# The head of a chunked scan taken pair by pair, with inputs and result laid out in DRAM as their tiles lie in SBUF

## The reference, cut to what matters

```
layer 0: x += gate * (linear recurrence over time of rmsnorm(mod(x)) @ B, @ C, + D)
         x += gate * score * expert[argmax](mod(x))             # 8 experts, 128 -> 256 -> 128
layer 1: q, k = silu(h Wq), silu(h Wk); v = h Wv                # h = mod(x); 16 heads of 64
         lr, wd = rates from sigmoid(h Wlr), sigmoid(h Wbeta), mean over a chunk
         for each of 8 chunks of 64 tokens:                     # carry W_in, W_out: 64 x 64 a head
             p_q, p_k = softmax(W_in q), softmax(W_in k);  o = p_q W_out
             G = gradient through the softmax of k with v and W_out
             W_out = W_out * wd_out + lr_out * p_k^T v;  W_in = W_in * wd_in + lr_in * G^T k
         x += gate * (o Wo)
         x += gate * top-2 of 8 experts (capacity 256, 128 -> 512 -> 128)
```

## Time and profile before

| | us |
|---|---|
| median of 3 runs | 822.17 (820.05 to 823.3) |
| the profiled execution | 820.11 |
| its span | 818.4 |
| TensorE busy | 706.1 (86%) |
| VectorE busy | 639.6 (78%) |
| POOL busy | 571.4 (70%) |
| ACT busy | 477.2 (58%) |

### The profile page before, as it was taken

How to read it: one execution, slowest core, us unless ns; L and a number is a source line. 1 busy time by engine, 2 the same in 40 slices (tenths; PEclk the granted TensorE clock), 3 DMA queues, 4 the chain that set the end, 5 groups by cost and what they waited for, 6 DMA issues and landing times.

```text
span 818.4 us, 34170 instructions
## 1 busy us (share of the span) xinstructions
PE 706.1 (86%) x14849; PEld 648.5 (79%) x14850; DVE 639.6 (78%) x1039; ACT 477.2 (58%) x764; POOL 571.4 (70%) x425
## 2 busy tenths in 40 slices
PE   4668677736989999999999999999999999786997
PEld 3358567736879999899988899889999888675897
DVE  5993754448879999899988999999998998866215
ACT  4745333424846775586767567666757765648510
POOL 4811177173778899889898988878888878732750
PEclk9775689959999999999999999999999999986999
DMA  9741354310060000000000000000000000062128
GB/s 230 199 108 39 78 120 97 74 48 13 24 191 8 10 8 7 7 6 11 7 6 7 20 2 3 11 10 3 4 16 4 4 17 16 4 206 77 51 78 274
DMA packets 60959, 42.89 MB, mean 52 GB/s; under 512 B 21776, under 2 KB 53664, under 8 KB 60816
## 3 DMA queue, kind: packets, MB, share of 16 engines
q1 hardware_dynamic: 57232, 34.00, 15.1%
q0 software_dynamic: 3296, 6.76, 3.7%
q10 hardware_dynamic: 288, 0.01, 0.0%
HBM read 26.65 MB, written 14.09 MB: 50 GB/s over the span
## 4 chain that ended last, share of the span: by engine, by line
PE 70%; issue 11%; DVE 7%; POOL 5%; ACT 4%; DMA 2%; DVEq 0%; POOLq 0%; ACTq 0%; SPq 0%
PE psum L1872 19%; PE psum L1927 8%; PE psum L1972 7%; PE psum L1905 7%; PE psum L1963 4%; PE psum L1920 4%; PE psum L1934 4%; PE psum L1942 3%; ACT arena L1064 2%; PE psum L1913 2%; PE psum L2223 2%; POOL arena L564 1%; PE psum L1810 1%; POOL y_rows L703 1%; PE psum L1736 1%
## 5 line engine op out<-in xcount | busy, mean ns | idle before, releaser
L1872 PE MATMUL psum<-hT,w_qkv 128*128 128x128 f32 x1408 | 173.4, 280 | 2.3 <-DVE arena L1418 1.9
L1872 PEld LDWEIGHTS psum<-hT,w_qkv 128*128 128x128 f32 x1408 | 164.2, 194 | 5.3 <-DVE arena L1418 2.1
L610 POOL TENSOR_TENSOR arena<-arena,small 128x1024 f32<-128x1024 f32 x56 | 106.0, 1914 | 48.9 <-DVE small L1431 48.9
L589 POOL TENSOR_TENSOR arena<-arena 128x1024 f32<-128x1024 f32 x56 | 106.7, 1905 | 13.0 <-ACT arena L947 12.4
L575 POOL TENSOR_TENSOR arena<-arena 128x1024 f32<-128x1024 f32 x56 | 106.5, 1902 | 0.0
L1424 DVE TENSOR_REDUCE small<-arena 128x16 f32<-128x1024 f32 x60 | 73.2, 1219 | 9.1 <-ACT arena L936 6.8
L614 POOL TENSOR_TENSOR arena<-arena 128x1024 f32<-128x1024 f32 x28 | 65.8, 2352 | 17.5 <-DVE arena L1451 17.5
L1412 DVE TENSOR_REDUCE small<-psum 128x16 f32<-128x1024 f32 x60 | 72.8, 1216 | 2.2 <-PE psum L1972 2.2
L916 ACT ACTIVATE arena<-psum 128x1024 f32<-128x1024 f32 x28 | 28.7, 1025 | 72.4 <-PE psum L1872 72.4
L1418 DVE TENSOR_TENSOR arena<-psum,small 128x1024 f32<-128x1024 f32 x60 | 70.5, 1215 | 0.1
L1905 PE MATMUL psum<-arena 64*128 64x64 f32 x1344 | 61.5, 230 | 8.1 <-issue 6.7
(11 more groups left out here) (323 smaller groups left out, 1620.9 us busy)
## 6 DMA issues: line engine op xcount, KB each, us to landing
y_rows<-hT SPq DMA_DIRECT2D x8, 512.0 KB
arena<-y_rows SPq DMA_DIRECT2D x8, 512.0 KB, 7.3
o_rows<-arena SPq DMA_DIRECT2D x9, 256.0 KB
x_sb<-in_L_attn_u SPq DMA_DIRECT2D x8, 256.0 KB, 6.0
arena<-in_W_inT SPq DMA_DIRECT2D x16, 128.0 KB
arena<-in_W_out SPq DMA_DIRECT2D x64, 32.0 KB
h_rows<-arena SPq DMA_DIRECT2D x4, 512.0 KB, 3.5
h_rows<-hT SPq DMA_DIRECT2D x8, 256.0 KB, 2.3
```

The source lines that it names most:

```text
L589: pool.tensor_tensor(x3, x3, lr[:, tile_of(t) * 32 + k * H:tile_of(t) * 32 + k * H + H].unsqueeze(2).to_broadcast([P, H, D]), ALU.mult).th ...
L610: pool.tensor_tensor(z4, z4, r3.unsqueeze(3).to_broadcast([P, 8, 2, CH]), ALU.mult).then_inc(done, 1)
L1872: mm = pe.matmul(ps[bank][:, p * P:(p + 1) * P], w_qkv[:, j * HD + p * P:j * HD + (p + 1) * P], hT[:, at:at + P], start=True, stop=True)
```

## The change

In DRAM, x, the result, both layers' expert weights, w_o and the scan's initial states now lie as their tiles lie in SBUF, so that a row of a partition is one run; the host lays them out and turns the result back. That makes 4 DMAs of the 8 for x, 8 of the 80 for the states, 1 of the 4 for w_o, and 8 of the 16 for the result.

The head of the scan takes pair 0 of group 0 alone as soon as its own gather has landed (`first_back`) and the other three pairs together after it. Norm and modulation of group 0 move from ACT to VectorE. ACT makes two roots (pair 0, pairs 1 to 3), loads the Tanh table, and goes on with tanh; group 1's root comes one turn later with a table load on either side. TensorE runs 12 warm-up products, then interleaves transposes and products. The k product of step 1 goes to another PSUM bank (`k_bank`), so it need not wait for step 0's logits to be read. POOL takes over `group_take` of groups 1 and 2, issues 12 instead of 16 gathers ahead of its loop, and two each in turns -1 to 2 behind the normalisations. Group 1's transposes, hT, tokens and sums come one turn later (`early_of`).

```diff
+        def early_of(i, ahead, n=NC):
+            return 1 if i + ahead == 5 else group_of(i, ahead, 2, n)
+        def rows_in(c):
+            return c // 2 * 64 + (64 if c % 2 else 48)
+        def k_bank(t):
+            return 0 if t == 1 else 3
...
@@ sync
             def load_x(bp):
-                for be in range(2):
-                    sp.dma_start(x_sb[be * CH:(be + 1) * CH, bp * W8:(bp + 1) * W8].rearrange("p (t c) -> p t c", c=C),
-                                 A["L0_attn_u"][2 * bp + be].rearrange("(t p) c -> p t c", p=CH)).then_inc(x_in[bp], 16)
+                sp.dma_start(x_sb[:, bp * W8:(bp + 1) * W8], A["x_rows"][:, bp * W8:(bp + 1) * W8]).then_inc(x_in[bp], 16)
...
+            sp.dma_start(w_o[:, :], A["Wo_rows"]).then_inc(a1_w, 16)
             def load_w_in(bp):
+                sp.dma_start(w_in[bp], A["W_in_rows"]).then_inc(w_set, 16)
             def load_w_out(bp):
+                sp.dma_start(w_out[bp], A["W_out_rows"]).then_inc(w_set, 16)
...
+                half = slice(n * (W8 // 2), (n + 1) * (W8 // 2))
+                sp.dma_start(A["out"][:, half], x_sb[:, half]).then_inc(out_sem, 16)
@@ gpsimd
+            def group_take(c):
+                b3, x3, gates = group_tiles(c)
+                pool.wait_ge(group_taken, c)
+                pool.wait_ge(back_in[c % 2], rows_in(c))
+                chain.link(pool.tensor_tensor(b3, b3, tile_scores(c), ALU.mult))
+                chain.link(pool.tensor_tensor(b3, b3, gates, ALU.mult))
+                pool.tensor_tensor(x3, x3, b3, ALU.add).then_inc(group_taken, 1)
-            for n in range(4 * BP):
+            for n in range(2 * BP):
                 gather_back(n)
+            group_take(1)
+            for n in range(2 * BP, 3 * BP):
+                gather_back(n)
+            group_take(2)
...
             for i in range(-1, TU - 1):
-                if i + 17 < T:
+                if 3 <= i and i + 17 < T:
                     gather_back(i + 17)
...
                 normalise_p(i + 1, 0, pq_norm)
                 normalise_p(i + 1, 1, pk_norm)
+                if i < 3:
+                    gather_back(2 * i + 14)
+                    gather_back(2 * i + 15)
@@ scalar
+            act.activation(junk, ln_eps, ACT.Sqrt)
+            first_root(0, 1, 1)
+            first_root(1, BP, 2)
+            act.activation(junk, ln_eps, ACT.Tanh)
+            q_tanh(0); k_tanh(0); group_tanh_of(0); q_tanh(1); k_tanh(1); exponentials(0, 0)
...
+                if i == 0:
+                    group_root(1)
+                    act.activation(junk, ln_eps, ACT.Tanh)
@@ vector
+            dve.wait_ge(first_back, 16)
+            chain.link(first_take(0, 1))
+            first_measure(0, 1); first_norm(0, 1); first_hT_of(0).then_inc(group_hT, 1)
+            dve.wait_ge(back_in[0], rows_in(0))
+            first_take(1, BP).then_inc(group_taken, 1)
+            first_measure(1, BP); first_norm(1, BP); first_hT_of(1).then_inc(group_hT, 1)
+            q_silu(0); first_hT_of(2); first_hT_of(3).then_inc(group_hT, 1)
+            k_silu(0); q_silu(1); maxima(0, 0); group_rates_out(0); maxima(0, 1)
+            centre(0, 0); centre(0, 1); k_silu(1); group_measure(1)
+            add_up(0, 0); add_up(0, 1); invert(0); group_rate(1)
@@ tensor
+            keep_warm(12, ps[1][:, 0:P])
+            first_turn(0); pe.wait_ge(group_hT, 1); project(0, 0, 1, pe_pq)
+            first_turn(1); project(0, 1, 3, pe_pk); first_turn(2); first_turn(3)
+            pe.wait_ge(group_hT, 2); pe.wait_ge(silu_q, 1); project(1, 0, 1, pe_pq); group_tokens(0)
+            pe.wait_ge(silu_k, 1); logits_of(0, 0); group_sum(0); logits_of(0, 1)
+            pe.wait_ge(group_rates, 1); project(1, 1, k_bank(1), pe_pk)
+            pe.wait_ge(z_centered, 1); pe.wait_ge(silu_q, 2); pe.wait_ge(silu_k, 2); logits_of(1, 0)
+            pe.wait_ge(z_centered, 2); logits_of(1, 1)
+            for i in range(2, TZ):
+                turned, tokens, summed = early_of(i, 2), early_of(i, 1, NC - 1), early_of(i, 0, NC - 1)
```

More of the change, by code:

```diff
@@ L997, in group_score @@
                 last.then_inc(group_scored, 1)
[L999 removed]
+            act.activation(junk, ln_eps, ACT.Sqrt)
+            first_root(0, 1, 1)
+            first_root(1, BP, 2)
+            act.activation(junk, ln_eps, ACT.Tanh)
+            q_tanh(0)
+            k_tanh(0)
+            group_tanh_of(0)
+            q_tanh(1)
+            k_tanh(1)
+            exponentials(0, 0)
+            for i in range(0, TU + 1):
                 if 0 <= i - 1 < TU:
                     k_tok_out(i - 1)
[L1002 to L1004 removed]
+                exponentials(i, 1)
+                if 1 <= i and i + 1 < TZ:
                     k_tanh(i + 1)
[L1006 to L1007 removed]
+                if i == 0:
+                    group_root(1)
+                    act.activation(junk, ln_eps, ACT.Tanh)
                 if 0 <= i - 1 < TU:
@@ L1466, in gate_y @@
                 dve.tensor_tensor(y_gated, y_bank(t), rows1(GA, t % BP), ALU.mult).then_inc(y_scaled, 1)
-            group_take(0)
-            group_measure(0)
-            group_rate(0)
-            group_take(1)
-            group_measure(1)
-            group_take(2)
-            for i in range(-3, TU - 1):
+            dve.wait_ge(first_back, 16)
+            chain.link(first_take(0, 1))
+            first_measure(0, 1)
+            first_norm(0, 1)
+            first_hT_of(0).then_inc(group_hT, 1)
+            dve.wait_ge(back_in[0], rows_in(0))
+            first_take(1, BP).then_inc(group_taken, 1)
+            dve.wait_ge(group_taken, 1)
+            first_measure(1, BP)
+            first_norm(1, BP)
+            first_hT_of(1).then_inc(group_hT, 1)
+            q_silu(0)
+            first_hT_of(2)
+            first_hT_of(3).then_inc(group_hT, 1)
+            k_silu(0)
+            q_silu(1)
+            maxima(0, 0)
+            group_rates_out(0)
+            maxima(0, 1)
+            centre(0, 0)
+            centre(0, 1)
+            k_silu(1)
+            group_measure(1)
+            add_up(0, 0)
+            add_up(0, 1)
+            invert(0)
+            group_rate(1)
+            for i in range(-1, TU - 1):
                 if i >= 0:
@@ L2253, in layouts @@
     a["L1_b1_cols"] = t(np.asarray(inputs["L1_ffn_b1"]).reshape(E, F1 // P, P), 2, 0, 1).reshape(P, -1)
-    a["W_inT"] = t(w_in, 1, 2, 0)
-    a["W_out"] = t(w_out, 1, 0, 2)
+    twice = lambda x: np.ascontiguousarray(np.concatenate([x.reshape(P, -1)] * 2, axis=1))
+    a["W_in_rows"] = twice(w_in.reshape(D, HP, 2, D).transpose(2, 3, 1, 0))
+    pairs = w_out.reshape(D, 2, 2, 2, 2, D).transpose(3, 4, 0, 1, 2, 5)
+    a["W_out_rows"] = twice(np.stack([np.stack([pairs[q ^ r, r] for r in range(2)], axis=3) for q in range(2)]))
+    wo = t(inputs["L1_attn_Wo"], 1, 0).reshape(4, 2, 2, D, C).transpose(1, 2, 3, 0, 4)
+    a["Wo_rows"] = np.ascontiguousarray(np.stack([np.stack([wo[q ^ r, r] for q in range(2)], axis=1) for r in range(2)]).reshape(P, HP * C))
+    for l in range(2):
+        a[f"L{l}_W1_rows"] = t(inputs[f"L{l}_ffn_W1"], 1, 0, 2).reshape(P, -1)
+        w2 = np.asarray(inputs[f"L{l}_ffn_W2"])
+        a[f"L{l}_W2_rows"] = t(w2.reshape(E, -1, P, C), 2, 0, 1, 3).reshape(P, -1)
+    a["x_rows"] = t(np.asarray(inputs["L0_attn_u"]).reshape(BP, 2, NC, CH, C), 1, 3, 0, 2, 4).reshape(P, T * C)
     return a
```

266 lines of the change are left out of this document (114 added, 152 removed).

## The result

The changed kernel takes 814.62 us (four runs, 812.83 to 815.39) where the kernel before takes 821.97 beside it (820.05 to 823.3): ratio 0.9901, 95% interval 0.9873 to 0.9929, faster by 7.35 us. On another chip the same pair gave 0.9879 (0.9846 to 0.9912). The forecast was 817.0 in a range of 810 to 821.5.

The account below looks back on a forecast made before the run. TensorE was taken to bound the scan's steps and latency its start; -1.3 -0.6 -0.7 -2.8 +0.5 +0.6 = -4.3 gave 815.8 or 817.9 by base, and the forecast was set at 817.0, range 810 to 821.5.

Parts of the forecast that it names:

- First loads: Kernel start: one DMA per input pair lets the weights TensorE waits for land sooner, -1.3 us (bounds 0.7 and 2.0).
- Initial states: First layer's gathers: 80 state DMAs become 8, so SP's queue no longer slows a gather, -0.6 us (bounds 0 and 1.2).
- Last store: Kernel end: 16 DMAs become 8, one issue fewer behind the last addition, -0.7 us (bounds 0.3 and 1.2).
- Head, the gain: Scan start: VectorE begins after the first pair's gather; step 0's logits 6.3 us earlier, step 1's 7.4 earlier.
- Given back, first part: VectorE before step 1's maxima: group 1's moments, sums and rate, plus 1.3 us contention, cut the gain to 5.0.
- Given back, second part: Group 3's late gathers hold ACT for 3 us, with hT behind; the gain shrinks from 4.7 to about 1 at k_silu(3).
- Third, the stall: TensorE's 3.70 us stall before the transposes at 233.05 falls partly into an existing wait: -2.8 us (bounds 1 and 5).
- Rival A: Scan head: early start survives, gathers 14 and 15 land before ACT asks and the stall goes; 813 us, chance 0.30.
- Fourth: POOL's first four turns: eight gathers issued where it issued four, +0.5 us (bounds 0 and 2.6).
- tokens: Group 1's tokens and sums move one turn later, into one where TensorE is full, +0.6 us (bounds 0 and 1.6).
- Rival B: Front: big loads back to back fill the DMA engines and instructions come late; slower, 826 us, chance 0.08.
- Rival C: Front's gain is lost in VectorE's chain and the stall keeps its length; -1.7 in all, 820.5 us, chance 0.20.

Follow-up runs that it names:

- the vector first: Changed kernel with group 3's gathers ahead of POOL's taking of group 2 and the conditioning vector first in the inputs' queue: ratio 0.9902 to the kernel before.
- the layouts alone: Kernel before with the new loads and stores and the old head, against the kernel before: ratio 0.9964 on the second chip, 0.9979 on the fourth.
- the gathers ahead: Changed kernel with group 3's gathers issued ahead of POOL's taking of group 2, against the kernel before: 0.9825 (second chip), 0.9846 (fourth, 805.15 us).
- the head alone: Changed kernel with the old loads and stores, against the kernel before: ratio 0.9859 on the second chip, 0.9924 on the third.

## Why the prediction was right, and where its terms were off

**First loads, -1.3.** Too large. The columns moved from 7.90 to 7.32 on the first chip and not at all on the fourth (7.31 and 7.32). In all traces they start at 6.94 to 7.90 with the old loads and at 7.30 to 7.32 with the new, 7.58 with the vector first. At the states' reading no lead beyond the spread between traces is left. The step that failed is the assumption that issues and packets in front of the weights set their landing: the weights now go out at 1.27 instead of 2.28, and on the fourth chip neither the load of the weights into TensorE (7.29 against 7.31) nor the columns started sooner.

**Initial states, -0.6.** The queue's hold of 10.39 is gone, but of the lead of 2.12 at the first expert gather (97.69 to 95.57, fourth chip) 2.27 arrive at the first return gather, so this stage gave 0.15. A gather of 1.46 to 1.48 stands some 8 us behind the first one in every trace from the first, third and fourth chip, with the new loads too (at 103.5 to 105.6): the 1.48 of the earlier trace rows had nothing to do with SP's sixteen issues.

**Last store, -0.7.** 1.0, in each trace with the new layout. I had an issue gone and no change in what one costs; it fell from 0.616 to 0.333 as well. The three terms sum to -2.6, and the layouts alone measured -3.1 and -1.7. The sum fits, but of its terms the traces bear out only this one.

**Head, the gain.** First product 6.6 earlier forecast, 6.55 in the first pair of traces; logits of step 0 6.3 against 6.5; logits of step 1 7.4 against 8.1. These steps hold, and so does the 12.50 to 6.11 and 6.25 of the fourth chip.

**Given back, first part.** Forecast 5.0 at the k product of step 2, found 8.0. The 5.0 itself isn't what the listed terms give: 1.25, 2.4, 0.7 and 1.3 sum to 5.65, which would leave 1.8 of the 7.4, and the prediction shows no working for the difference. Two terms were wrong. VectorE's moments and sums, which I counted as new work in front of the maxima, fell into time in which VectorE had been idle before: 1.12, 0.48 and 1.92 us,

```profile
199.87 1.23 DVE L1412 TENSOR_REDUCE small<-psum 128x16 f32<-128x1024 f32 x1 [1.12 <-PE psum L1972]
201.57 1.23 DVE L1412 TENSOR_REDUCE small<-psum 128x16 f32<-128x1024 f32 x1 [0.48 <-PE psum L1972]
206.98 1.22 DVE L1424 TENSOR_REDUCE small<-arena 128x16 f32<-128x1024 f32 x1 [1.92 <-ACT arena L936]
```

which is the kernel before, waiting twice for TensorE's logits of 2.90 and once for ScalarE. And the 1.3 for contention at the rate's last operation did not come, by 0.01 us of order (0.16 at 189.40). The Trainium skill (GPSIMD Engine Reference, section Specifications) has POOL contend with VectorE instructions of two SBUF inputs. The rows agree where POOL's operation was already running: 0.99 with the gathers ahead, 1.45 in the earlier trace rows. The rule was right and the order in time was not.

**Given back, second part.** The mechanism held, and the size of the hold: ScalarE was held 3.25 (forecast 3), hT followed, and from step 1's normalisation to k_silu(3) the lead fell from 8.1 to 3.0, by 5.1 where I had 3.7. k_silu(3) is 3.0 earlier, I had said 1. The run with the gathers ahead takes 3.0 of the loss away (56.28 against 59.24), which shows the cause.

**Third, the stall.** This is the term that was mis-sized. I had the transposes 2.8 earlier, on the ground that part of TensorE's stall would fall into a wait that is there anyway. They came 6.1 earlier in the first trace (67.78 to 61.65 from the first return gather), since VectorE's lead of 3.0 and the stall's 3.70 added up, less 0.6 that they now start further behind their operand. The upper bound of 5 was too low as well. And nothing was counted for the lower clock behind the stall, 1.2 us up to the logits of step 3. Rival A's reason (TensorE passes before the writes flow) doesn't fit: the writes began at 212.35, 9.7 ahead of the transposes, about as before (10.3). Why TensorE has no such stall with the new head is open: in eight of nine traces with it there is none over 1 us up to step 3's logits, and in the ninth one of 1.88 in a place where the old head had none. In the trace of after a packet of instructions ended at 220.25, 1.8 ahead of the transposes at 222.09, so there it was in time; the one that ended at 225.79 was not, and behind it came the stall of 1.88. TensorE's program is another one with the new head, which no run separates.

**Fourth, +0.5, and tokens +0.6.** No run separates them. POOL is busier by 8 us in the whole span (571.4 to 579.5) and the head alone still nets 6.2.

**The sum.** In two parts the forecast was layouts -2.6 and head -1.7 (-2.8 +0.5 +0.6). Measured: layouts -1.7 and -3.1, head -6.2 on the third chip, whole -7.35 on the first. The result came 2.4 under the forecast because the head kept more than I gave it, near Rival A's 813, though not by A's way: the hold of ScalarE was there. Rival B fell: no product of TensorE waits over 1 us under the name issue in the first 60 us. Its weight loads do, 5.1 where it was 4.7, at a place where the product beside them waits for POOL; it is 5.1 in the second trace of before too. Rival C fell with the head alone.

That 817.0 lies as near as it does is partly luck. The early terms were too large (-1.9 for first loads and states, of which the traces show 0.6 and 0.15 at most), the stall's was too small (-2.8 against 6.1), and in the one pair of traces from the first chip the head's lead of 7.4 at the logits of step 3 is gone by the last projection (548.64 and 548.95), which no term foresaw.

## What to carry to other kernels

A wait that precedes another isn't simply subtracted from it: to size a stall that no operand explains, take it away in the kernel before (here by spreading the writes around it, worth 0.9967 by itself) and only then sum. Look in the list of DMA queues for the packet of instructions ahead of it, and count the lower clock behind it too (here 1.2 us on top of 2.7). When work is moved ahead of a point, look for the idle time that it will fill; 3.5 us of "new" work on VectorE cost nothing here because VectorE had stood still for as long in the same turn. And when gathers are moved out of the way of a head, ask who needs the last of them: keeping group 3's ahead took ScalarE's wait of 3 us away and gave the fastest kernel of this study.

## What the runs showed of the hardware that I had not expected

One chip took 860 us for the kernel that takes 818 to 822 on the three others, and most of the time lies in one stage. With the layouts alone the first return gather was at 187.24 there and at 160.97 on the fourth chip: 26 of the 37 us between these two traces, with 4 more in the turns of the scan and 7 behind them, where the same kind of wait stands again. At 111 to 126 us three engines stood still together, ScalarE and VectorE with their inputs long made, TensorE behind VectorE:

```profile
121.49 1.14 ACT L828 ACTIVATE arena<-psum,route 128x128 f32<-128x128 f32 x4 [10.39 <-remote]
125.51 0.69 DVE L1283 COPY arena<-psum 128x512 f32<-128x512 f32 x1 [19.11 <-remote]
126.26 3.78 PE L1789 MATMUL psum<-arena 128*128 128x128 f32 x16 [13.63 <-DVE arena L1283]
187.24 0.99 POOL L529 DMA_INDIRECT arena<-o_rows,route  x1 [29.50 <-DMA o_rows<-arena]
```

All four kernels run there did so and none on the other chips; what they waited for the trace doesn't name. Comparisons with this chip's times would have been worthless.

Two traces of one kernel (after, and the whole change on the third chip) are 9 us apart between the second turn and the last, 480.1 and 471.0, with 456.38 and 454.97 us of TensorE's work in them:

```profile
229.00:709.00 480.00, 456.38 (x12269) 425.66 (x12264) 438.39 (x537) 321.10 (x411) 414.09 (x249) 1.00 0.03 8
226.00:697.00 471.00, 454.97 (x12273) 424.85 (x12265) 438.38 (x538) 321.14 (x411) 416.28 (x251) 1.00 0.04 11
```

The first 1.2 of it lie behind the stall of 1.88: there the clock was granted at 0.50 from 227.87 to 231.28, where the other trace has 1.00. For the rest no single wait holds the difference; it grows by a little in most of the turns. From the first pair of traces alone one would say that the head's lead was lost in the turns. The runs of the head alone say it was not. Whether the 9 us belong to the first chip or to the execution stays open.
